# Unit pipeline one tick longer, PSUM dealt out anew, the front of a group over seven ticks

## The reference

```
x = x + attention(ada_ln(x, c), ada_ln(ctx, c)) @ Wp + bp            # CROSS0
x = x + gate_a * (attention(modulate(ln(x)), same) @ W_proj + b)     # SELF1
x = x + attention(ln(x), ln(ctx)) @ W_cproj + b                      # CROSS1
x = x + gate_m * (gelu(modulate(ln(x)) @ W1 + b1) @ W2 + b2)         # MLP
```

## Time and profile before

| | |
|---|---|
| three runs | 348.48, 348.33, 347.09 us, median 348.33 us |
| the profiled execution | 346.47 us, its span from first to last instruction 344.6 us |
| mean granted TensorE clock | 0.953 of full |
| busy share of the span | PE 82%, DVE 72%, ACT 60%, POOL 38% |

### The profile page before, as it was taken

How to read it: one execution, slowest core, us unless ns; L and a number is a source line. 1 busy time by engine, 2 the same in 40 slices (tenths; PEclk the granted TensorE clock), 3 DMA queues, 4 the chain that set the end, 5 groups by cost and what they waited for, 6 DMA issues and landing times.

```text
span 344.6 us, 10197 instructions
## 1 busy us (share of the span) xinstructions
PE 283.7 (82%) x3827; PEld 181.3 (53%) x3827; DVE 247.7 (72%) x631; ACT 206.1 (60%) x324; POOL 130.7 (38%) x257
## 2 busy tenths in 40 slices
PE   0736549989899898998989889898897878879894
PEld 0413435656566565665655666555665555534342
DVE  6764795897887878778798787988879787613103
ACT  1324127676776756767676676676777667665540
POOL 8271942525225243153643646446352131301000
PEclk9975657999999999999999999999999999999998
DMA  6952311313131322323323233132231300000013
GB/s 193 306 140 57 91 49 50 93 49 90 55 95 49 94 68 77 80 64 95 83 64 96 56 87 95 52 93 66 80 95 52 95 3 4 5 0 2 1 30 91
DMA packets 31904, 25.39 MB, mean 74 GB/s; under 512 B 4552, under 2 KB 31600, under 8 KB 31856
## 3 DMA queue, kind: packets, MB, share of 16 engines
q1 hardware_dynamic: 30240, 23.49, 25.3%
q10 hardware_dynamic: 1616, 1.25, 1.2%
HBM read 4.41 MB, written 1.05 MB: 16 GB/s over the span
## 4 chain that ended last, share of the span: by engine, by line
PE 43%; DVE 26%; issue 15%; POOL 5%; ACT 4%; DMA 4%; SPq 1%; ACTq 1%; POOLq 0%; DVEq 0%
DVE normed L751 7%; PE attn_ps L426 7%; PE misc_ps L359 7%; PE keyed_ps L408 4%; DVE neg_max L770 4%; PE score_ps L473 4%; DVE stats L735 4%; PE keyed_ps L462 4%; DMA stack_q<-max_rows 4%; PE score_ps L384 3%; PE misc_ps L436 3%; PE misc_ps L367 3%; DVE rest L762 2%; PE misc_ps L343 2%; ACT parts L584 2%
## 5 line engine op out<-in xcount | busy, mean ns | idle before, releaser
L770 DVE TENSOR_REDUCE neg_max<-score_ps 128x8 f32<-128x1024 f32 x96 | 117.0, 1219 | 14.8 <-PE score_ps L384 14.8
L604 ACT ACTIVATE probs<-keyed_ps 128x1024 f32<-128x1024 f32 x96 | 98.3, 1024 | 12.7 <-PE keyed_ps L408 10.4
L426 PE MATMUL attn_ps<-probs,values 128*32 128x128 f32 x1536 | 62.0, 279 | 0.4 <-ACT probs L604 0.4
L408 PE MATMUL keyed_ps<-stack_q,stack_k 64*128 64x128 bf16 x768 | 38.6, 220 | 10.2 <-DMA stack_q<-max_rows 9.1
L426 PEld LDWEIGHTS attn_ps<-probs,values 128*32 128x32 f32 x1536 | 36.2, 109 | 19.9 <-issue 11.3
L904 POOL TENSOR_TENSOR rstd<-var_eps,minus_half 128x4 f32<-128x4 f32 x24 | 24.4, 1016 | 56.5 <-DVE var_eps L740 56.3
L384 PE MATMUL score_ps<-stack_k,stack_q 62*128 62x128 bf16 x768 | 38.8, 221 | 7.0 <-DVE neg_max L770 7.0
L911 POOL CAST max_parts<-neg_max 128x16 bf16<-128x16 f32 x48 | 10.2, 212 | 89.4 <-DVE neg_max L770 89.3
L570 ACT ACTIVATE normed_t<-misc_ps,mod 128x128 f32<-128x128 f32 x48 | 18.0, 456 | 33.1 <-PE misc_ps L349 24.2
L621 ACT ACTIVATE attn_t<-misc_ps,bcol 128x128 f32<-128x128 f32 x48 | 17.7, 368 | 32.3 <-PE misc_ps L441 30.8
L408 PEld LDWEIGHTS keyed_ps<-stack_q,stack_k 64*128 64x128 bf16 x768 | 21.9, 95 | 24.5 <-DMA stack_q<-max_rows 14.7
(11 more groups left out here) (94 smaller groups left out, 400.0 us busy)
## 6 DMA issues: line engine op xcount, KB each, us to landing
stack_q<-parts SPq DMA_DIRECT2D x72, 128.0 KB, 2.4
stack_k<-parts SPq DMA_DIRECT2D x72, 128.0 KB, 2.4
stack_q<-max_rows SPq DMA_DIRECT2D x96, 4.0 KB
xs<-in_x_dram SPq DMA_DIRECT2D x4, 256.0 KB, 6.3
cs<-in_ctx_dram SPq DMA_DIRECT2D x4, 256.0 KB, 6.3
out_dram<-xs SPq DMA_DIRECT2D x4, 256.0 KB, 2.3
w<-in_L_xcond_W_mlp_dram SPq DMA_DIRECT2D x2, 256.0 KB, 4.4
wmod<-in_L_xcond_W_mod_dram ACTq DMA_DIRECT2D x1, 384.0 KB, 4.7
```

The lines of the kernel that those rows point to most:

```text
L408: mm = pe.matmul(keyed_ps[:, e, a * T:(a + 1) * T], stack_k[rows, g % STACKS, CP * c + a, cols], stack_q[rows, g % STACKS, CP * c + a, col ...
L426: mm = pe.matmul(attn_ps[at:at + QUAD, slot * T:(slot + 1) * T], values[:, u // PER % STACKS, u % PER, h, :], probs[:, n % 3, (CP * e + a) ...
L604: act.activation(probs[:, n % 3, :], keyed_ps[:, :, :].rearrange("t e n -> t (e n)"), ACT.Exp, scale=float(D) ** -0.5).then_inc(probs_read ...
L770: dve.tensor_reduce(neg_max[:, u % 2, :, CP * c:CP * (c + 1)], score_ps[:, :, :].rearrange("t e (a k) -> t e a k", k=T), AX.X, ALU.max, ne ...
```

## The change

- Scores run three units ahead in place of two (`AHEAD = 3`). turn_max, copy_max_rows and move_max work on unit t + 2 in place of t + 1; turn_attn and attn_with_bias on unit t - 2 in place of t - 1.
- PSUM: `way_in_ps`, one bank, holds both the sums (attn_ps, 256 columns) and their transposes (out_ps, 256 columns). `turn_ps`, one bank, holds in turn the transposed maxima, attn turned and the output projection. `ring_ps`, two banks, serves the fronts, the gates and the MLP (`take_ring`, as take_misc, but two uses back).
- values holds two heads in 32 columns, one in the first 16 and one in the last; two matmuls add into the same 32 partitions. So the sums of a unit fill 256 columns in place of 512, and two transposes in place of four turn them.
- attend's first half waits also for `attn_ready` of the unit before. turn_max and turn_attn wait for branch_added, turn_attn for max_row_ready as well.
- The front's steps lie one to a tick over seven ticks. Semaphores of the norms are kept apart for x and context. modulate is cut in two halves around the second exponential.
- Gates are made for two batches at a time in eight ticks from 16 to 31 (GATES_AT), behind attend. FIRST is -11 in place of -10. The MLP's steps have ticks of their own (UP_AT, DOWN_AT, TURN_AT) and each does its four matmuls in a block.

```
-MISC = 3
+HALFQ = 16
+AHEAD = 3
+RING = 2
...
-        attn_ps = stack.enter_context(nc.psum_tensor("attn_ps", [128, 512], F32))
-        misc_ps = stack.enter_context(nc.psum_tensor("misc_ps", [128, MISC, 512], F32))
+        way_in_ps = stack.enter_context(nc.psum_tensor("way_in_ps", [128, 512], F32))
+        turn_ps = stack.enter_context(nc.psum_tensor("turn_ps", [128, T], F32))
+        ring_ps = stack.enter_context(nc.psum_tensor("ring_ps", [128, RING, 512], F32))
+        attn_ps = way_in_ps[:, 0:2 * T]
+        out_ps = way_in_ps[:, 2 * T:4 * T]
+        max_row_ps = turn_ps[0:2 * HEADS, 0:T // 2].bitcast(BF16)
...
+        UP_AT, DOWN_AT, TURN_AT = (48, 49, 50, 52), (49, 50, 52, 53), (50, 51, 53, 54)
+        GATES_AT = (16, 19, 20, 23, 24, 27, 28, 31)
@@ attend(u, c), its first half @@
                     pe.wait_ge(summed_ready, u)
-                for a in range(CP):
-                    for e in range(2):
-                        h = 2 * (CP * c + a) + e
-                        at, slot = QUAD * (h % 4), h // 4
-                        mm = pe.matmul(attn_ps[at:at + QUAD, slot * T:(slot + 1) * T],
-                                       values[:, u // PER % STACKS, u % PER, h, :],
-                                       probs[:, n % 3, (CP * e + a) * T:(CP * e + a + 1) * T], start=True, stop=True)
+                    pe.wait_ge(attn_ready, u)
+                for e in range(2):
+                    for a in range(CP):
+                        mm = pe.matmul(attn_ps[QUAD * a:QUAD * (a + 1), c * T:(c + 1) * T],
+                                       values[:, u // PER % STACKS, u % PER * PAIRS + CP * c + a, 2 * e:2 * e + 2, :],
                                        probs[:, n % 3, (CP * e + a) * T:(CP * e + a + 1) * T],
+                                       start=(e == 0), stop=(e == 1))
@@ turn_attn(u) @@
+                pe.wait_ge(max_row_ready, min(u + 5, UNITS))
+                if u >= 1:
+                    pe.wait_ge(branch_added, u)
@@ the loop of VectorE @@
-                if unit(tick + 2):
-                    row_max(tick + 2, 0)
-                if unit(tick + 1):
-                    copy_max_rows(tick + 1)
+                if unit(tick + AHEAD):
+                    row_max(tick + AHEAD, 0)
+                if unit(tick + 2):
+                    copy_max_rows(tick + 2)
...
+                if unit(tick + AHEAD):
+                    row_max(tick + AHEAD, 1)
+                if q is not None:
+                    leave_rest(q, 0)
+                if k is not None:
+                    leave_rest(k, 1)
                 if unit(tick - 2):
                     add_branch(tick - 2)
                 if unit(tick - 1):
                     divide(tick - 1)
-                if unit(tick + 2):
-                    row_max(tick + 2, 1)
```

More of the change, by code:

```diff
@@ L189, in batches, with front @@
             return b, b + PER
[L192 to L196, removed]
+        def front(tick, step, n=0):
+            g, left = divmod(tick + 10 - step, PER)
+            if left or not 0 <= g < GROUPS + MLP_GROUPS:
+                return None
+            if n == 1 and layer(g) not in (CROSS0, CROSS1):
+                return None
+            return g
@@ L206, in at_tick @@
[L206 to L212, removed]
@@ L214, in build @@
-        MISC_ORDER = [("cond",), ("mod",), ("bias",)] + [use for tick in range(FIRST, LAST) for use in at_tick(tick)]
+            norm_x, norm_c, q = front(tick, 2), front(tick, 3, 1), attention(front(tick, 3))
+            k, v = attention(front(tick, 4)), attention(front(tick, 5))
+            return ([("norm", norm_x, 0)] * (norm_x is not None) + [("norm", norm_c, 1)] * (norm_c is not None)
+                    + [("k", k)] * (k is not None) + [("v", v)] * (v is not None) + [("q", q)] * (q is not None)
+                    + [("gate", i) for i in range(B // 2) if GATES_AT[i] == tick] + [("late",)] * (tick == 0) + [("mlp", i) for i in range(4) if TURN_AT[i] == tick])
@@ L221, in build, with ring @@
[L221 to L227, removed]
+                   "v": lambda g: (v_ready, g + 1), "gate": lambda i: (gate_ready, i + 1), "mlp": lambda q: (mlp_gated, q + 1)}
+        def ring(*use):
+            return ring_ps[:, RING_ORDER.index(use) % RING, :]
@@ new lines, in _ @@
+                if norm_c is not None:
+                    transpose_normed(norm_c, 1)
+                if k is not None:
+                    project_qk(k, 1)
+                if v is not None:
+                    project_v(v)
+                if unit(tick):
+                    keyed_scores(tick, 1)
+                if unit(tick - 2):
+                    turn_attn(tick - 2)
+                if unit(tick - 1):
+                    turn_summed(tick - 1)
+                if unit(tick + AHEAD):
+                    scores(tick + AHEAD, 1)
@@ L516, in _ @@
                 if unit(tick):
                     attend(tick, 0)
[L518 to L520 removed]
+                if tick in GATES_AT:
+                    gates(GATES_AT.index(tick))
+                if tick == 0:
                     late_modulations()
[L522 to L527 removed]
@@ L528, in _ @@
-                if 0 <= q - 2 < 4:
-                    turn_mlp(q - 2)
+                if tick in DOWN_AT:
+                    for c in range(MLP):
+                        mlp_down(DOWN_AT.index(tick), c)
+                if tick in UP_AT:
+                    for c in range(MLP):
+                        mlp_up(UP_AT.index(tick), c)
+                if tick in TURN_AT:
+                    turn_mlp(TURN_AT.index(tick))
         @block.scalar
@@ new lines, in modulate @@
+                if first:
+                    act.wait_ge(normed_ps[n], nth(g, n) + 1)
+                    if g >= 1 and s < LAYERS:
+                        act.wait_ge(v_ps, g)
+                        act.wait_ge(qk_ps, 2 * g)
+                    if g == 0:
+                        act.wait_ge(mod_ready, 2)
+                    if s == SELF1:
+                        act.wait_ge(mod_ready, 5)
+                ps = ring("norm", g, n)
+                js = range(PER // 2) if first else range(PER // 2, PER)
@@ L574, in first_part @@
+                if not first:
+                    last.then_inc(normed_t_ready[n], 1)
             def first_part(g, n):
@@ L640, in _ @@
             for tick in range(FIRST, LAST):
[L641 removed]
+                norm_x, norm_c = front(tick, 2), front(tick, 3, 1)
+                q, k = attention(front(tick, 4)), attention(front(tick, 5))
                 if unit(tick):
@@ L949, in _ @@
             for tick in range(FIRST, LAST):
-                g0, g1, g2, g3 = (front_at(tick, i) for i in range(4))
-                norm = (g0, 0) if g0 is not None else (g1, 1) if (g1, 1) in NORMS else None
+                stats_c, stats_x = front(tick, -1, 1), front(tick, 0)
+                q, k = attention(front(tick, 4)), attention(front(tick, 5))
+                if unit(tick + 2):
+                    split_max(tick + 2)
                 if unit(tick - 3) and (tick - 3) // B == SELF1:
```

380 lines of the change are left out of this document (185 added, 195 removed).

## The result

The changed kernel takes 438.38 us, the median of four runs (435.29 to 442.94), against 348.4 us before (four runs, one more than in the table above): 1.256 times as long, with a 95% interval of 1.247 to 1.265. Medians count every run; the ratios leave out runs more than 1.5% above the fastest of the same kernel, so the two differ a little. The forecast was 408 us, with 435 as its upper end. The profiled execution took 435.29 us, its span is 433.5 us.

What follows compares the result with a forecast made beforehand. Waits between TensorE and VectorE were taken to bound the kernel. Ticks adding 61 us to the 344.6 us span, with start and tail netting 0, gave 406; 1.9 above span made 408 us, range 375 to 435.

Steps and rivals of the forecast that it cites:

- The ring: Attend waits for VectorE's division, behind a row max needing TensorE's second scores: 1.65 us stall, 5.60 us per plain tick.
- 1.6 us a time, some 45 times, 70 us or more: Sign in the profile: attend waiting for VectorE's division, in all 70 us or more, as TensorE's largest wait.
- The two old waits: TensorE's waits for the max rows by DMA (9.1 us) and for normalised rows (15.2 us) were to vanish.
- The granted clock at 1.00 between 60 and 390 us: Sign in the profile: TensorE's clock stays full, 2.4 GHz, through that stretch.
- The clock falls, 440 to 500: Rival: idle TensorE drops to 1.2 GHz, adding 80 to 95 us, half that if it swings; chance 0.08.
- The replayed ticks: Ticks rebuilt from old trace spacings: 5.60 us plain, 5.83 with transposes, 6.92 with k or v, before POOL's extra 0.5.
- The max transpose behind POOL: TensorE's max transpose waits for POOL's split of the maxima: 0.5 us more in two of four ticks.
- Gates: Eight pairs in ticks 16 to 31, behind attend, cost TensorE 1.2 us each: 9.6 us.
- The rest on the ring: VectorE's rest subtraction, between row max and division in ticks with k or v, adds 0.7 us of spacing each.
- They are worth nothing extra: Halved summed transposes (14 us, already counted) and vanished waits bring nothing further, since TensorE has time in the stall.
- The tail: After the units, the MLP in blocks of four ups with its last turn later: +1 us, between -2 and +5.
- The rival "faster": Attend's wait does not bite, which needs a division ahead of the second row max: 310 to 320 us, chance 0.06.

Runs made afterwards that it cites:

- ring alone: Kernel before, with attend's first half waiting for the previous unit's division, placed behind the second row max; banks, fronts and pipeline unchanged: 411.49 us, 1.180 times.
- 16 fillers: Changed kernel plus 16 constant matmuls a tick ahead of attend's first half, results overwritten: 415.85 us, 1.198 times the kernel before.
- Moving the split: Changed kernel with POOL's split of the maxima right after the row max, ahead of the rest splits: 415.05 us, 1.193 times the kernel before.
- split and fillers: Changed kernel with POOL splitting the maxima early and 16 constant matmuls a tick ahead of attend's first half: 398.63 us, 1.147 times the kernel before.
- The division first: Changed kernel with VectorE's division of unit t-1 moved ahead of the second row max of its tick: 405.96 us, 1.172 times the kernel before.
- 4 fillers: Changed kernel with 4 constant matmuls a tick ahead of attend's first half, about 0.2 us of work: 424.34 us, 1.222 times the kernel before.

## Why the prediction was wrong

- **Direction and cause** were right. The ring is there, between the instructions that were named, and alone makes 64 us (ring alone). Attend's wait was to be "1.6 us a time, some 45 times, 70 us or more": it is 81.1 us in 47 times. The stalls fit tick by tick: 1.68 us in the ticks with x's transposes (1.65 replayed), 2.34 with a rest subtraction (1.65 + 0.7), 0.82 with a q projection (1.65 - 0.98). The two old waits are no longer among the large ones. The 64 us of the ring alone hold the lower clock that comes with it (0.91).
- **The step that failed** is in the list of what would show each step: "The granted clock at 1.00 between 60 and 390 us". The clock's cost was put at nothing in the sum, and only priced as a rival ("The clock falls, 440 to 500", half of its loss "if it swings") at 0.08. The profile has 0.89 from 60 to 340 us. The evidence that I set against it, 300 to 310 us at 73% busy and full clock, was one stretch of ten microseconds. The fillers settle it: holding the clock at 0.98 gives 415.9 us. From tick 4 to the last keyed scores the changed kernel takes 302.2 us, with 16 fillers 281.1: 21 us for the clock. The rival's price was too high in turn: half of its 80 to 95 us is twice what the swing cost (and would give 448 us and more, not its 440), so that 438 us lies in none of the ranges.
- **Where the 30 us lie** that the forecast lacks: 22 in the ticks (336.5 against 314.4 us), 2 at the start (49.3 against 47.2), 4 in the tail (47.7 against 44.0) and 3 between the profiled execution and the median, which the prediction left aside. Inside the ticks two errors go against each other. Ticks 0 to 3 take 34.3 us where the replay has 26.5, 8 more. The ticks behind them, 302.2 against 287.9, are 14 more: 21 for the clock, less 7 by which the replay was too long at full clock (281.1 with the fillers).
- **The replayed ticks** were right to a few per cent each: 5.68 us measured against 5.60 at full clock. With the split early and the clock held, ticks with k take 6.75 us (6.92 replayed), those with v 6.78 without gates (6.92), those with x's transposes, tick 0 and gates aside, 5.64 to 6.06 (5.83). That the whole comes within 1% (302.7 against 304.4) is in part luck: ticks 0 to 3 are 2 us longer than replayed, 27.8 against 25.5, and the rest 4 us shorter.
- **The max transpose behind POOL**, 10 us, measured 11.1 us of waits, but not where it was put: three waits up to tick 0 (1.5, 2.4 and 2.4) were left out of it, one in tick 3 is 1.9 where it has 0.5, and the other eight, in ticks with v or x's transposes, are up to 0.38 us each, where it has 0.5 in twenty ticks. Moving the split gave 23 us without fillers and 17 with them (415.9 to 398.6).
- **Gates**, "now behind attend and so fully on the ring: 9.6 us": 6.5 us came back. In the ticks with v the pair then has to wait for the rest subtraction, 6.2 us in all, so this run alone does not bound the term. The tick lengths of the run with split and fillers do in part: a tick with v takes 6.78 us without and 7.84 with a pair of gates behind attend, 1.06 for a pair where I took 1.2.
- **The rest on the ring**, 0.7 us in 20 ticks, 14 us: attend's wait fell by 12, the time by 9.
- **"They are worth nothing extra"**, of the gains: right for the changed kernel. Even in the kernel before, the halved transposes bring 1 to 3 us of 14.
- **The tail**, +1: it is +4.7. Between the last keyed scores and the MLP's first matmul lie 7.2 us, against 5.0 in the kernel before, and 40.5 against 38.0 behind that. In the first piece the last 32 matmuls of attend take 1.94 us; with the clock held and the split early they take 1.08, and the piece is 4.9 us. The division first, with the same blocks of the MLP, has 4.0 and 40.7. So about half of the surplus is the clock and the ring in the last units, and the other half stays with the MLP; what its blocks or its waits cost was not tried apart. (In the two runs with 16 fillers the second piece is longer, 42.3 and 42.5 us, for a reason not followed.)
- **The rival "faster"** named the right place ("a division ahead of the second row max"), and was wrong that this alone would do: the second ring through POOL stood behind it and left 406 us.

What stays open: why ticks 0 to 3 take 8 us more than replayed, which was not tried apart beyond the waits for POOL; why the same stalls bring the clock down in some ticks and not in others; and whether the new wait could be done without in another layout of the banks, which wasn't tried.

## What to carry to other kernels

When two tiles are put into one bank, the new wait is cheap or dear by where its releaser stands in its own engine's order: look for a path from the waiting instruction's predecessors through the other engine back to it. If there is one, replay a tick with the spacings of the old trace; here that gave the ticks at full clock within some per cent. Then ask what the stall does to the clock, and put that into the sum, not among the rivals. And a ring that is cut may only uncover the next, so count the second longest as well.

## What the hardware did that I had not expected

TensorE stood idle ahead of attend for 0.5 to 2.3 us in 47 of 48 ticks, and the granted clock swung between 2.4 and 1.2 GHz: a mean of 0.89 from 60 to 340 us is 62 us at the lower level. Yet it stayed at 1.00 from 210 to 240 us with the same stalls. Matmuls of constants, whose results nobody reads, made the kernel 22.5 us faster. The Trainium skill (TensorE: Matmul & The Clock Gate, "A second HAM failure mode: psum-queue depth-cycling") tells of a kernel that idles a little between groups of matmuls, and whose clock swings by it; the trace agrees, with 0.89 for the mean clock between 60 and 340 us. The changed kernel also spreads more between runs, 435 to 443 us, where the kernel before has 347 to 349. That the swinging clock does this isn't shown: with 4 fillers the clock swings too (0.92), and the four runs lie between 423 and 426 us.
